# The prologue of an adaLN layer kernel rebuilt: rows of the modulation in two parts, statistics of x taken ahead, a PSUM bank for each chunk, softplus in halves

## What is computed

```python
mod = (silu(c) @ wmod).reshape(8, 6, 1, 256)
sa, ca, ga, sb, cb, gb = mod rows;  ga, gb = sign * max(abs, 0.25)
h = layernorm(x) * (1 + ca) + sa
x = x + ga * block(h)          # Mamba
h = layernorm(x) * (1 + cb) + sb
x = x + gb * experts(h)        # 8 experts, best 2 of each token, softmax weights

def block(h):
    xn = h * rsqrt(mean(h * h) + eps) * norm_w
    xi, z = split(xn @ W_in)                       # 256 -> 512, 512
    xc = silu(causal_conv4(xi) + conv_b)
    dt, B, C = split(xc @ W_x)                     # 512 -> 64, 16, 16
    dt = softplus(dt @ W_dt + b_dt)
    state[t] = exp(dt * A) * state[t-1] + (dt * xc) * B[t]    # 16 states for each of 512 channels
    y = sum_s state * C + D_skip * xc
    return h + (y * silu(z)) @ W_out
```

## Time and profile before

| | us |
|---|---|
| median of three runs | 1826.16 (1823.35 to 1827.03) |
| the profiled execution | 1823.74 |
| its span, first to last instruction | 1821.0 |
| first scan | 91.8 |
| end of stage A | about 1214.9 |
| VectorE busy in the span | 1330.2 (73%) |
| PE busy | 1354.1 (74%) |
| GpSimd busy | 999.6 (55%) |
| ScalarE busy | 903.0 (50%) |

### The profile page before, as it was taken

How to read it: one execution, slowest core, us unless ns; L and a number is a source line. 1 busy time by engine, 2 the same in 40 slices (tenths; PEclk the granted TensorE clock), 3 DMA queues, 4 the chain that set the end, 5 groups by cost and what they waited for, 6 DMA issues and landing times. The chain is left out here.

```text
span 1821.0 us, 27625 instructions
## 1 busy us (share of the span) xinstructions
PE 1354.1 (74%) x7872; PEld 1095.3 (60%) x7873; DVE 1330.2 (73%) x2554; ACT 903.0 (50%) x1326; POOL 999.6 (55%) x858
## 2 busy tenths in 40 slices
PE   2666677676676776676776775617999999999995
PEld 0244455454454454464554464517899999999994
DVE  1297997997898997998998998645555555555552
ACT  2567757657657756756756756312222222222220
POOL 2187768668667687687685778220233333333331
PEclk7788897898888898888798888855999999999997
DMA  4211110410400411411310310233742232223224
GB/s 128 87 43 63 40 36 19 133 41 19 133 29 33 122 36 36 119 38 36 100 40 24 105 41 18 75 122 117 210 99 52 52 57 55 52 53 59 53 52 113
DMA packets 85590, 124.87 MB, mean 69 GB/s; under 512 B 12712, under 2 KB 59432, under 8 KB 85232
## 3 DMA queue, kind: packets, MB, share of 16 engines
q1 hardware_dynamic: 68400, 91.85, 16.3%
q0 software_dynamic: 16128, 28.39, 8.3%
q10 hardware_dynamic: 960, 3.46, 0.6%
HBM read 96.98 MB, written 30.88 MB: 70 GB/s over the span
## 5 line engine op out<-in xcount | busy, mean ns | idle before, releaser
L450 POOL TENSOR_TENSOR dBu<-u,brep 128x512 f32<-128x512 f32 x512 | 637.6, 1277 | 134.3 <-DVE hs L975 70.4
L975 DVE TENSOR_TENSOR_SCAN hs<-psum,dBu 128x512 f32<-128x512 f32 x512 | 608.4, 1208 | 68.3 <-ACT psum L597 58.1
L771 PE MATMUL psum<-ident,hs 128*128 128x128 f32 x2048 | 324.7, 310 | 201.5 <-DVE y L986 156.7
L597 ACT ACTIVATE psum<-dt,aneg 128x512 f32<-128x512 f32 x512 | 347.5, 688 | 227.9 <-DVE hs L975 224.2
L771 PEld LDWEIGHTS psum<-ident,hs 128*128 128x128 f32 x2048 | 262.1, 158 | 289.0 <-DVE y L986 207.7
L1408 ACT ACTIVATE w_now<-w_sb 128x2048 f32 x72 | 137.5, 1911 | 391.7 <-PE psum L1430 381.6
L1390 POOL DMA_INDIRECT sum_d<-ysb,row_of_sum x72 | 114.2, 1586 | 335.5 <-DVE ysb L1496 332.5
L1430 PE MATMUL psum<-xgT,w_now 128*128 128x128 f32 x2304 | 273.3, 278 | 0.0
L780 PE MATMUL psum<-ident,hc 128*128 128x128 f32 x1024 | 186.6, 315 | 113.8 <-ACT hc L583 74.9
L1430 PEld LDWEIGHTS psum<-xgT,w_now 128*128 128x128 f32 x2304 | 267.1, 194 | 0.2
L1441 PE MATMUL psum<-w_sb,hT 128*128 x1152 | 260.4, 379 | 0.0
(11 more groups left out here) (163 smaller groups left out, 1340.1 us busy)
## 6 DMA issues: line engine op xcount, KB each, us to landing
brep<-b_d SPq DMA_DIRECT2D x128, 256.0 KB, 3.2
w_sb<-in_W SPq DMA_DIRECT2D x16, 1024.0 KB
xin<-in_x SPq DMA_DIRECT2D x8, 512.0 KB, 7.0
h_d<-hmod SPq DMA_DIRECT2D x8, 512.0 KB, 3.0
modo<-mod_d SPq DMA_DIRECT2D x8, 512.0 KB, 5.9
xres<-in_x SPq DMA_DIRECT2D x8, 512.0 KB, 6.8
hres<-h_d SPq DMA_DIRECT2D x8, 512.0 KB, 7.4
xhat_d<-modo SPq DMA_DIRECT2D x8, 512.0 KB, 3.5
```

Source lines behind the costliest of these rows:

```text
L450: nc.gpsimd.tensor_tensor(dBu[:, i % RING, :], u[:, p, c, :], brep[:, s % 4, :], ALU.mult).then_inc(s_dBu, 1)
L597: nc.scalar.activation(dA[:, i % DA_RING, :], dt[:, p, c, :], ACT.Exp, scale=aneg[:, c, s:s + 1]).then_inc(s_dA, 1)
L771: last = nc.tensor.transpose(T[:, i // DT, c * P:(c + 1) * P], hs[:, s % 2, c, i * P:(i + 1) * P], ident[:, :])
L975: nc.vector.tensor_tensor_scan(hs[:, s % 2, c, :], dA[:, i % DA_RING, :], dBu[:, i % RING, :], 0.0, ALU.mult, ALU.add).then_inc(s_scan, 1)
```

## The change

The prologue and what feeds it are written anew; the expert stages aren't touched.

- The four large weights are loaded from ScalarE's queue; SP loads c, wmod, x of sequences 0 and 1 and the small weights. A first activation table is chosen so that silu, copies and squares need no other.
- The first copy of modulation rows is stored at once when VectorE has added 1 to the second row (512 columns), and read back; the clamped rows are stored behind that in a second transfer. `clamped` does the six operations for one row.
- x of sequences 2 to 7 is loaded in the prologue into halves of `u`, `dt` and `sz` that sequence 1 will use later (`xs_of`), and statistics are taken from there (`x_stats`): 0 to 3 in the prologue, 4 to 7 behind steps 7 to 10 of sequence 0. `p_stats` and `ln1` leave all bodies; GpSimd does the rstd of several sequences at once. x itself is still loaded again for the normalising.
- h of sequence 0 is modulated on VectorE instead of GpSimd; squares and norm of sequence 1 move into steps 0 and 1 of sequence 0, its rms to GpSimd behind the first four dBu.
- Sequence 0 has a PSUM bank for each chunk of xi (and then of dt) and for each chunk of z. silu of a chunk follows its taps; x_proj takes chunk by chunk. xnT is scaled on VectorE.
- Softplus of sequence 0: max(v, 0) is on VectorE, Ln, sum and product are in two halves, and decays and dBu of a half wait for that half alone.
- `o_base` no longer adds the two weights and no longer scales `xf`. `base` on GpSimd multiplies `xf` by the gate row (128x1024) and adds it; SP's store waits for the weights only (`s_wts`).

The core of the diff (changes that only rename semaphores or shift counts are left out):

```diff
+        def two_of(t):
+            return [t[:, 1, 2 * k:2 * k + 2, :].rearrange("p c l -> p (c l)").rearrange("p (i d) -> p i d", d=D) for k in range(2)]
+
+        xs_of = [xin[:, :, :], two_of(xc)[0], *two_of(u), *two_of(dt), *two_of(sz)]
...
+        X0_PS = PS[:, 0:4, :]
+        Z0_PS = (PS[:, 6, :], PS[:, 7, :], Q[:, 1, :], Q[:, 0, :])
...
+            sp.dma_start(xin[:, :, :], x[0:L, :].rearrange("(i p) d -> p i d", p=P)).then_inc(s_xin, 16)
+            sp.dma_start(xs_of[1], x[L:2 * L, :].rearrange("(i p) d -> p i d", p=P)).then_inc(s_x1st, 16)
+            for dst, src in ((nw[:, :], norm_w), (cw[:, :, :], conv_w), (cb[:, :], conv_b), (bdt[:, :], b_dt),
+                             (dsk[:, :], D_skip), (aneg[:, :, :], A_log),
+                             (wg[:, :, :], Wg.rearrange("(k p) n -> p k n", p=P))):
                 sp.dma_start(dst, src).then_inc(s_w, 16)
             sp.wait_ge(s_modr, 1)
-            sp.dma_start(mod_d, m8).then_inc(s_modst, 16)
+            sp.dma_start(mod_d[:, 0:2 * D], m8[:, 0:2 * D]).then_inc(s_modst, 16)
...
             def prologue():
-                load(0)
-                load(1)
+                sp.dma_start(**mod_rows(0, 0, 2, modp[:, :, :])).then_inc(s_modp, 16)
+                for n in range(2, NB):
+                    sp.dma_start(xs_of[n], rows(x, n)).then_inc(s_xst, 16)
                 store_h(0)
+                sp.dma_start(**mod_rows(1, 0, 2, modp[:, :, :])).then_inc(s_modp, 16)
+                sp.wait_ge(s_modr, 2)
+                sp.dma_start(mod_d[:, 2 * D:6 * D], m8[:, 2 * D:6 * D]).then_inc(s_modst, 16)
...
             def base(n):
-                pool.wait_ge(s_scaled, n + 1)
+                pool.wait_ge(s_xh, n + 1)
+                nc.gpsimd.tensor_tensor(xf[:, :, :], xf[:, :, :], modo[:, 3, :].unsqueeze(1).to_broadcast([P, TI, D]), ALU.mult).then_inc(ol, 1)
+                pool.wait_ge(ol, 8 * n + 8)
...
-                for n in range(2):
-                    ln1(n)
-                    p_mod(n)
-                    rms(n)
+                ln1(0, 1, 0)
+                ln1(1, 1, 1)
+                rms(0)
+                p_mod(1)
+                ln1(2, 2, 2)
...
                         gate(n - 1, 1 - p)
-                    if has_r and s == 4:
-                        ln1(n + 2)
+                    if not has_o and s == 0:
+                        rms(1)
+                    if not has_o and s == 12:
...
         @block.scalar
         def _(act):
+            for dst, src in ((win[:, :, :], W_in.rearrange("(k p) n -> p k n", p=P)),
+                             (wx[:, :, :], W_x.rearrange("(k p) n -> p k n", p=P)),
+                             (wdt[:, :], W_dt), (wout[:, :, :], W_out.rearrange("(k p) n -> p k n", p=P))):
+                act.dma_start(dst, src).then_inc(s_w, 16)
+            nc.scalar.preload_act_table_set("silu_and_others")
             act.wait_ge(s_ct, 32)
             nc.scalar.activation(cts, cts, ACT.Silu).then_inc(s_csilu, 1)
-            nc.scalar.preload_act_table_set("natural_log_exp_and_others")
...
             def prologue():
-                p_norm(0)
+                mod_copy(0)
+                act.wait_ge(s_xin, 16)
+                p_norm(0, xin, 0, lambda i: slice(i, i + 1))
+                mod_copy(1)
+                mod_copy(2)
                 squares(0)
...
+                act.wait_ge(s_x1st, 16)
+                p_norm(1, xs_of[1], 1, lambda i: slice(TI + i, TI + i + 1))
+                act.wait_ge(s_w, 16 * 11)
...
+                silu_first(0)
+                conv_first(2)
+                silu_first(1)
+                conv_first(3)
+                silu_first(2)
+                act.wait_ge(s_modst, 32)
+                silu_first(3)
                 exps_again()
+                z_first(0)
+                decay_rates()
                 xd_copy(0)
                 c_copy(0, 0)
-                for c in range(CH):
-                    softplus_in(0, 0, c)
-                softplus_ln(0, 0)
-                for c in range(CH):
-                    z_in(0, 0, c)
-                squares(1)
-                norm(1)
+                for half in range(2):
+                    for c in (2 * half, 2 * half + 1):
+                        act.wait_ge(s_dtp, c + 1)
+                        nc.scalar.activation(u[:, 0, c, :], X0_PS[:, c, :], ACT.Abs, bias=bdt[:, c:c + 1]).then_inc(s_act, 1)
+                        act.wait_ge(s_act, 2 * c + 1)
+                        nc.scalar.activation(u[:, 0, c, :], u[:, 0, c, :], ACT.Exp, scale=-1.0).then_inc(s_act, 1)
+                    act.wait_ge(s_act, 4 * half + 4)
+                    nc.scalar.activation(u[:, 0, 2 * half:2 * half + 2, :], u[:, 0, 2 * half:2 * half + 2, :], ACT.Ln,
+                                         bias=1.0).then_inc(s_sp0, 1)
+                for c in range(1, CH):
+                    z_first(c)
...
-                    in_proj_x(0, c, c % 2, PAD * (c - 1))
-                x_proj(0, 0)
+                    for k in range(DC):
+                        last = nc.tensor.matmul(X0_PS[:, c, :], win[:, k, c * P:(c + 1) * P], xnT[:, k, :],
+                                                start=(k == 0), stop=(k == DC - 1))
+                    last.then_inc(s_xip, 1)
+
+                def z_first(c):
+                    for k in range(DC):
+                        last = nc.tensor.matmul(Z0_PS[c], win[:, k, DIN + c * P:DIN + (c + 1) * P], xnT[:, k, :],
+                                                start=(k == 0), stop=(k == DC - 1))
+                    last.then_inc(s_zp, 1)
+
+                for c in range(3):
+                    z_first(c)
+                for c in range(CH):
+                    pe.wait_ge(s_xc0, c + 1)
+                    last = nc.tensor.matmul(Q[0:XD, XB, :], wx[:, c, :], xc[:, 0, c, :],
+                                            start=(c == 0), stop=(c == CH - 1))
+                last.then_inc(s_xdp, 1)
+                pe.wait_ge(s_tap, CH * PAD)
+                pe.wait_ge(s_xd, 1)
+                for c in range(2):
+                    nc.tensor.matmul(X0_PS[:, c, :], wdt[:, c * P:(c + 1) * P], xd[0:R, :], start=True, stop=True).then_inc(s_dtp, 1)
                 c_t(0)
-                for c in range(CH):
-                    dt_proj(0, c)
-                for c in range(CH):
-                    in_proj_z(0, c)
+                for c in range(2, CH):
+                    nc.tensor.matmul(X0_PS[:, c, :], wdt[:, c * P:(c + 1) * P], xd[0:R, :], start=True, stop=True).then_inc(s_dtp, 1)
+                pe.wait_ge(s_c, 1)
+                z_first(3)
...
                 nc.vector.tensor_copy(w1, vd[:, 2, :])
-                nc.vector.tensor_copy(w2, vd[:, 1, :])
...
-                link(nc.vector.tensor_tensor(vd[:, 3, :], vd[:, 1, :], vd[:, 2, :], ALU.add), "o", n)
-
-                dve.wait_ge(s_xh, n + 1)
-                for i in range(TI):
-                    last = nc.vector.scalar_tensor_tensor(xf[:, i, :], xf[:, i, :], vd[:, 3, i:i + 1], modo[:, 3, :],
-                                                          ALU.mult, ALU.mult)
-                last.then_inc(s_scaled, 1)
+                nc.vector.tensor_copy(w2, vd[:, 1, :]).then_inc(s_wts, 1)
 
             def prologue():
-                for n in range(2):
-                    p_stats(n)
-                    counted(P_LINKS, 0)
+                dve.wait_ge(s_xin, 16)
+                x_stats(0)
+                dve.wait_ge(s_m8, 1)
+                nc.vector.tensor_scalar(m6[:, 1, :], m6[:, 1, :], 1.0, None, ALU.add).then_inc(s_modr, 1)
+                dve.wait_ge(s_x1st, 16)
+                x_stats(1)
+                dve.wait_ge(s_m8, 3)
+                then(clamped(2))
+                then(nc.vector.tensor_scalar(m6[:, 4, :], m6[:, 4, :], 1.0, None, ALU.add))
+                dve.wait_ge(s_hn, 1)
+                dve.wait_ge(s_modp, 16)
+                h = hmod[:, :, :]
+                then(nc.vector.tensor_tensor(h, h, modp[:, 1, :].unsqueeze(1).to_broadcast([P, TI, D]), ALU.mult))
+                nc.vector.tensor_tensor(h, h, modp[:, 0, :].unsqueeze(1).to_broadcast([P, TI, D]), ALU.add).then_inc(s_h, 1)
+                clamped(5).then_inc(s_modr, 1)
+
+                dve.wait_ge(s_w, 16 * 11)
+                dve.wait_ge(s_xntp, 1)
+                for c in range(DC):
+                    last = nc.vector.tensor_scalar(xnT[:, c, :], Q[:, c, :], nw[:, c:c + 1], None, ALU.mult)
+                last.then_inc(s_xnt, 1)
                 for c in range(CH):
-                    conv(0, 0, c, c % 2)
-                dt_sum(0, 0)
-                dt_x(0, 0)
+                    dve.wait_ge(s_xi, c + 1)
+                    for k in range(PAD):
+                        late = PAD - k
+                        if k > 0:
+                            dve.wait_ge(s_tap, c * PAD + k)
+                        nc.vector.scalar_tensor_tensor(xc[:, 0, c, late:], X0_PS[:, c, 0:L - late], cw[:, c, k:k + 1],
```

(17 more changed lines are left out.)

254 lines of the change are left out of this document (146 added, 108 removed).

## The result

| | before | after |
|---|---|---|
| median of runs, us | 1826.6 (4 runs, 1823.35 to 1828.40) | 1802.17 (4 runs, 1796.49 to 1804.19) |
| profiled execution, us | 1823.74 (span 1821.0) | 1802.19 (span 1799.4) |
| ratio | | 0.9868, 95% interval 0.9853 to 0.9883 |

The change saves 24 us, not the 43 forecast. I cut both spans at the same places. "First y" is VectorE's first addition of outputs to `y` in a sequence, and a step of a sequence is counted from one such pair of additions to the next. e10 is a second trace of the changed kernel and gives an idea of the spread between runs.

The account below looks back on a forecast made before the run. VectorE was taken to bound stage A, up to about 1215 us, and PE the rest. -26.0 + 6.9 - 23.2 - 0.3 = -42.6 took 1823.74 to 1781.1; half of 2.4 added, rounded up: 1783 us, range 1770 to 1799.

Parts of the forecast that it names:

- What bounds the kernel: VectorE bounds stage A, PE the rest; microseconds taken from VectorE's list inside a sequence come off nearly whole.
- Start to first scan, -26.0: Prologue: a chain through all engines gets shorter link by link, first scan at 65.7 instead of 91.83 us.
- the 2.3 taken: Prologue: half of 1.83 MB of weights goes ahead of wmod and delays the first copy by 2.3 us.
- halves buy little: First softplus: VectorE waits for all four clamps; one Ln would start the scan within 1 us of the same time.
- Sequence 0, +6.9: Sequence 0: statistics of 4 to 7 add 6.9, those of 2 save 1.7, squares, norm and rms add 1.7 us.
- Later sequences, -23.2: Sequences 1 to 5 lose 1.7 us of statistics, 1 to 7 lose 2.1 of o_base's addition and scalings; -23.2 us.
- The port against the product: Rival, o_base: GpSimd's product goes first and VectorE waits 2.35 us in seven sequences; +16.5, 1799 us; chance 0.05.
- End of stage A, -0.3: End of stage A: GpSimd's product and addition delay VectorE's one-hot operations, leaving -0.3 us; -2.7 without the port.
- Slower: Rival, expert stage: denser work ahead lowers PE's clock; at 0.86 it costs 66 us, 1849 in all; chance 0.03.
- no saving on VectorE: Rival, later sequences: ScalarE's decays or PE are next, so the 23 us stay, 1806 us; chance 0.08.
- modulation late: Rival, prologue: weights go fully ahead of wmod and x loads delay a reload, 7 to 8 us, 1795; chance 0.12.
- The link to h: Prologue, start to h of the first sequence: h at 23.7 instead of 37.8 us, 14.1 us less.

Follow-up runs that it names:

- e10: The changed kernel itself, unaltered, traced and timed a second time beside runs of the kernel before; 0.9857 of before.
- e5: The changed kernel with VectorE's statistics of x put back behind step 1 of sequences 0 to 5, their result unread; 0.9920 of before.
- e8: The changed kernel with the first softplus in true halves: VectorE clamps, sums and multiplies one half before the next; 0.9854 of before.
- e15: The changed kernel with one Ln over all four chunks of the first softplus instead of two halves; 0.9882 of before.
- e14: The changed kernel without the statistics of sequences 4 to 7 in sequence 0, their tile set to one by memsets; 0.9849 of before.
- e2: The changed kernel, its two 4-element copies kept, with GpSimd's product waiting until VectorE has the tokens' weights ready; 0.9794 of before.
- e1: The changed kernel without VectorE's two 4-element copies, reciprocal and product writing the weights directly, GpSimd's product untouched; 0.9802 of before.
- e9: The changed kernel with weight loads on SP's queue behind the first reload, and h's two operations ahead of VectorE's small ones; 0.9866 of before.
- e7: The changed kernel with the four weight loads on SP's queue behind x of the first two sequences, not ScalarE's; 0.9860 of before.
- e12: The changed kernel with e1, e2, e8 and e9 together, and GpSimd held before step 13's dBu until the one-hot rows are written; 0.9721 of before.
- e13: e12 with the store of h and the second sequence's reload ahead of the six x loads on SP's queue; 1770.53 us, 0.9709 of before.
- e6: The changed kernel with ten VectorE instruction forms timed at the end of stage A, alone and beside a GpSimd product; run once, 1832.81 us.

## Why the prediction was wrong

*What bounds the kernel.* Right: VectorE's time inside a sequence counts (e5), 1.2 us for each 1.7.

*Start to first scan, -26.0.* Right, -25.5 and -24.5; in six more traces whose prologue is the same to the first scan it is -23.3 to -24.7. By its links in after: the silu at 10.21 is 2.4 late, as the 2.3 taken. The half behind this 2.3 was a choice, and partly lucky: the four weights are 1.90 MB and not 1.83, and 1.22 MB of them had gone by 10.2 us, more than half. The first copy is there at 14.7 (forecast 14.6). h is at 25.1 instead of 23.7, since both things it waits for are 1.5 us late: the reload took 4.5 us to land (22.0; 3.3 before), and the third copy ended at 20.1 (18.7), so VectorE's small operations at 22.5 (21.1). The product is at 33.65 (32.0), x_proj ends at 50.9 (49.8), softplus begins at 54.34 (53.5), the first scan is at 66.38 (65.7): half of what h had lost was made up on the way. One dBu gets in between the last half operations, as said, at 0.95 us instead of 1.3. That halves buy little is right: e8 and e15 have 1.1 and 0.9 us.

*Sequence 0, +6.9.* The mechanism was right. The measured +4.6 and +5.6 are lower, but nine traces with the same code there have +4.6 to +7.5, so the sum can't be called off. A term in it can: the four groups of statistics cost 3 to 4 us instead of 6.9 (e14). That leaves more for squares, norm and rms than the 1.7 taken. The fourth group lies in a wait that was there anyway.

*Later sequences, -23.2.* This step failed, in the term "the last addition and four scalings of o_base go ... 2.1 us", counted whole for seven sequences. VectorE no longer does this work, and GpSimd's product came right behind the last dBu, as the prediction said. But the prediction put the product's cost for VectorE at nothing, and gave the rival "The port against the product" a chance of 0.05. It asked only whether the small **product** would meet GpSimd's, and that one doesn't. The two copies behind it, which stand in its own list of VectorE's order, don't occur in it. The first of them waits for GpSimd's product and takes 2.17 us instead of 0.17: 7 times 2.0 to 2.1 is 14.3 us, as much as the 14.7 counted as gained. Step 11 takes 9.5 us in the mean of the seven sequences, 9.4 before. With GpSimd held (e2) it takes 7.6, 1.8 less than before where 2.1 were forecast, and the whole stretch is 18.7 us shorter than before, of 23.5 forecast; with the copies gone as well (e1) 20.3. The rival's price, 16.5 us and 1799 in all, was near: 1802 was measured.

Why the product passes and the copy doesn't is not shown. At 303.8 VectorE's product ends, GpSimd's starts at 303.76, and the copy, which waits for the product's semaphore, only at 303.96, so it may simply come too late. But the second one-hot compare of step 10, which waits for no semaphore, also takes 1.3 us instead of 0.18 in four of after's eight sequences, and 0.18 in the others.

A row of the kernel before could have warned, in step 10 of sequence 1, where GpSimd makes eight dBu in a row:

```profile
314.34 1.03 DVE L1028 TENSOR_TENSOR vd<-top 128x4 f32<-128x4 f32 x1
315.30 1.31 DVE L1030 CAST tif<-tix 128x8 f32<-128x8 uint32 x1
```

The cast has one input and takes 1.31 us, 0.17 at its shortest.

The statistics gave 1.3 us a sequence where 1.7 was forecast, 2 us in all. With the 14.3 of the copies this is 16 us, of the 18 and 15 that the third row of the table is short of the forecast.

*End of stage A, -0.3.* The mechanism is there:

```profile
1177.97 2.34 POOL L472 TENSOR_TENSOR x<-x,xf 128x1024 f32<-128x1024 f32 x1
1178.02 2.43 DVE L1143 TENSOR_TENSOR oh<-iota,tif 128x32 f32<-128x32 f32 x2
```

The one-hot pair takes 2.43 us instead of 0.29. With the port's wait of sequence 7 in it, the time from the first y of that sequence to the end of the stage went from 163.9 to 165.0 and, in e10, 162.8: no difference.

*What the profile after would show.* Right: first scan at 62 to 69; sequence 0 longer, though by 5 and not 7 us; x_proj at 50 (50.9); one dBu in between; no statistics on xin; the product right behind the last dBu. Late by 1.5 us: clamped rows and reload. Wrong: sequences 1 to 5 shorter by 3 to 4 us each (0.1 to 2.8 in after), stages behind shifted by 42 (26).

*Slower, no saving on VectorE, modulation late.* None came. The link to h gave 12.8 us of the 14.1 (37.86 to 25.11), and 15.9 in e9 (21.98). Taking the weights out of wmod's way is not enough by itself: in e7 the silu was 2.4 us sooner and h no sooner.

## What to carry to other kernels

Before work is moved from VectorE to GpSimd, list every VectorE instruction that can run beside it, not only those with two SBUF inputs: a copy, cast or scaling from SBUF to SBUF waited for GpSimd here as well, down to four elements for each partition, and the wait shows as busy time. The sign is a group whose shortest and median times are far apart. Small operations belong where GpSimd has been told to pause, or are written so that none is of these forms; here one wait more on GpSimd was worth 12 us, and a second one 8. Then look again at what GpSimd's later work meets: in e12 a third of what step 10 gained went to the dt sum. And when a link of a chain gets faster and the end doesn't move, look for what is queued in front of the next link, on its engine and in the queue that issues its transfers: in e9 a normalisation waited for a store that SP issued only when six loads were out.

The version that beats both is e13: 1770.53 us, 0.9709 (0.9687 to 0.9732) of before, 28 us less than the change by the ratios.

## What the runs showed of the hardware

- A copy of 128x4 in SBUF on VectorE took 2.17 us behind a GpSimd product of 2.35, 0.17 otherwise. Copy and scaling of 128x512 from SBUF waited for a GpSimd product; from PSUM they didn't; reciprocal, memset and scan didn't either (e6, e1).
- When VectorE and GpSimd both had work waiting behind a dBu, either could be next: VectorE's small product was (1.07 us), the copy linked behind it was not (303.96 against GpSimd's 303.76).
- From the issue of the 16 KB store of the rows to that of the reload it was 1.5 to 2.3 us in the traces with after's prologue and 5.0 in e7, where 1.90 MB of weights were loaded on the store's own queue ahead of it. The reload to 128 partitions, 256 KB, landed after 4.4 to 4.5 us, in e7 after 4.6, and after 5.0 in e9, where the weights were issued behind it.
- The same code behind stage A took 605.4 to 614.1 us. The granted clock 60 to 150 us into it was 1.00 in the shortest and 0.94 in the longest, but 607.7 us also came with 1.00.
